# A recurrence in groups of two in place of four, half of its normalising on POOL, statistics of x carried in rows, and half of x loaded in the head

## The chip, the cores and the metric

The kernel runs on one core of a Trainium2 chip. The metric is the device time of one execution in microseconds, the median of several. Engines are named as in the profile: PE (TensorE, with PEld its weight loads), DVE (VectorE), ACT (ScalarE), POOL (GpSimd) and SP (SyncE, which here only issues transfers).

## The reference

x has 8 sequences of 512 tokens with 128 channels, 4096 tokens. All is float32. Three sublayers follow one another:

```
x = x + 0.5 * moe(layernorm(x))
x = x + ssm(layernorm(x))
x = x + 0.5 * moe(layernorm(x))

moe:  probs = softmax(tokens @ gate_w)            # 8 experts
      e = argmax(probs); pos = place of the token among those of expert e
      tokens with pos < 160 go through relu(t @ w1[e]) @ w2[e], times probs[e]; the others give 0
ssm:  h[t] = W h[t-1] + B u[t]     # W: a rotation, circulant, its eigenvalues of modulus 1 from a_params
      y[t] = C h[t] + D * u[t]
```

An expert's weights are 128 x 512 and 512 x 128. At most 8 x 160 = 1280 tokens are changed by a moe sublayer, ten tiles of 128 rows.

## The kernel before

**Head (to about 25 us).** SP issues loads in order: x turned (channels on partitions) for the gates, then small weights, w1, w2. PE computes the gate's logits, DVE picks each token's expert and numbers the tokens (`mark`, `number`, `encode`), and `index` (L734) turns that into `tok`, the ten tiles' token numbers. DVE also works out the rotation's angles (`eigenvalues`) and, later, tables of their multiples by doubling (`powers`, L561; a level is four small operations in a chain).

**Experts, `slots(n)`, n = 0 and 1.** POOL gathers ten tiles of rows into `xg` (L370), one indirect transfer after another, and later scatters ten tiles of `xnew` (L381). Each engine follows a list of steps written out by hand (L271 to L284), and takes them strictly in order:

- PE: `i` transposes a gathered tile, `l` multiplies it with the gate (n = 0), `u` is an expert's first product, `d` its second, `o` transposes a tile of outputs back, `t` and `s` are the last expert's second product straight into rows; `x` are matmuls that only keep PE's clock up.
- DVE: `i` takes a tile's statistics, `l` and `f` are the two halves of the softmax, `d` copies an expert's output to SBUF, `o` writes `xnew` = output x gate + `xg` (L794), `p` is a level of `powers`.
- ACT: `i` copies a transposed tile, `u` is the relu, `g` and `e` are the logarithm and exponentials of the softmax.

In n = 0 there is one softmax for all ten tiles; in n = 1 two groups of five. Row tiles of outputs go to PSUM banks 2 and 3 in turn (`row_bank`). Meanwhile SP copies x to a scratch tensor `x1_scratch` in DRAM, one sequence after each gather (L305); the scatter writes the changed rows over it; then SP loads all of it into `x1` (L309).

**Recurrence.** The state is kept in the basis where W turns pairs of numbers by an angle, so that a sequence's recurrence becomes a running sum between a turn back and a turn forth. Tokens are taken in groups of TB = 4 neighbours (token 4p + c lies in row p, tile c), so that the sum runs over 128 groups. Per sequence b:

- DVE: `stats` (four `bn_stats`, four aggregations), `shift`; ACT: `deviation`; ACT normalises four tiles into `u` (L520); for b = 0 and 1 ACT takes two tiles and DVE two (L897).
- PE: `turn_u` transposes `u` (L1149), ACT copies it to `uT` (two buffers, L502); `group_sums` (L1158) sums each group in the eigenbasis into bank 5.
- ACT copies the two half planes crosswise to `vq` (L494, L495); DVE multiplies bank 5 with cosines into `va` (L842), POOL `vq` with sines into `vb` (L402); DVE scans their sum into `z` (L850); DVE and POOL turn forth, `zs` (L853) and `zc` (L409), and DVE adds them into `state` (L862).
- PE: `within_pairs` and `within_rest` (L1169 to L1184) add what tokens of the same group give each other, seven tables of 136 columns for the lags 0 to 3 and some gate columns; `read_out` (L1192) adds what the carried state gives. 128 channels and 8 gate columns per token leave together.
- DVE: `add_back` and `gate_back` (L867 to L881) add x and give the logits for the second moe; SP stores rows and output.

PE works in software pipeline: group sums of sequence i, read-out of i - 1, first half of within i, transposes of i + 1, second half of within i. DVE routes the first half of the tokens for the second moe during sequences 4 to 6 (`mark`, `number`, `encode`), the rest at the end (`gate_first` and after); `place` (L1031) and `index` close the stage. The last sequence's gate columns are computed ahead (`gates_within`, L1211, `gates_carried`, L1217).

Of the kernel before, what the change touches and what calls it, by code (L numbers as in the profile page):

```python
# [5 lines left out]
def macaron_moe_ssm_kernel(nc, x_in, x_turned, a_params, b_w, c_w, c_w_turned, d_skip, gate_w, w1, w2,  # L6
# [12 lines left out]
    NB, SEQ, D = x_in.shape  # L19
    E, _, F = w1.shape  # L20
# [3 lines left out]
    NG = SEQ // TB  # L24
    PITCH = D + E
    NT = T // P
# [20 lines left out]
    with ctx:  # L47
# [48 lines left out]
        x1 = sb("x1", [P, NT, D])  # L96
# [46 lines left out]
        xnew = sb("xnew", [P, NS, D])  # L143

        om = sb("om", [P, 4])
        c1 = sb("c1", [P, TB + 1])
        s1 = sb("s1", [P, TB + 1])
# [3 lines left out]
        xj = sb("xj", [P, TB, D])  # L151
        xj_part = sb("xj_part", [P, TB, D])
        vt = sb("vt", [P, TB, P])
        gg = sb("gg", [P, 2, PITCH])
        gt_part = sb("gt_part", [P, TB, PITCH])
        gt = sb("gt", [P, TB, PITCH])
        eye_gate = sb("eye_gate", [P, PITCH])
        tab = sb("tab", [P, E + TB * PITCH])
        tab0 = sb("tab0", [P, PITCH + E])
        lgu = sb("lgu", [P, TB, E])  # L160
        sstat = sb("sstat", [P, 2, TB, 6])
        smv = sb("smv", [P, 2, TB, 2])
        sln = sb("sln", [P, 2, TB])
        ssd = sb("ssd", [P, 4, TB])
        srs = sb("srs", [P, 2, TB])
        snb = sb("snb", [P, 2, TB])
        u = sb("u", [P, 2, TB, D])
        uT = sb("uT", [P, 2, SEQ])
        tg = sb("tg", [P, TB, 2, TB * E])
        vq = sb("vq", [P, NG])  # L170
        va = sb("va", [P, NG])
# [3 lines left out]
        zs = sb("zs", [P, NG])  # L175
        state = sb("state", [P, 2, NG])

        x1_dram = nc.dram_tensor("x1_scratch", [T, D], F32, kind="Internal").ap()
# [15 lines left out]
        d_fill = sem("d_fill")  # L194
        d_gather = [sem(f"d_gather{j}") for j in range(NS)]
# [46 lines left out]
        def y_of(b):  # L242

            return y_pair(b)[:, :, E:E + 2 * PITCH].rearrange("p h (r c) -> p h r c", c=PITCH)
# [7 lines left out]
        def row_bank(i):  # L252

            return 1 if i == NS - 1 else 2 + i % 2
# [10 lines left out]
        GROUPS = [[(0, NS)], [(0, NS // 2), (NS // 2, NS)]]  # L265

        def group(n, i):
# [3 lines left out]
        pe_steps = [steps("i0 x1 i1 x2 u0 i2 l0 l1 d0 i3 u1 i4 l2 u2 i5 l3 d1 i6 l4 l5 u3 i7 i8 l6 "  # L271
                         "l7 i9 l8 l9 d2 u4 o0 o1 d3 u5 o2 o3 d4 o4 u6 o5 d5 u7 o6 d6 t8 o7 s8 o8 t9"),
                    steps("i0 x1 i1 x2 u0 i2 u1 i3 d0 i4 u2 i5 d1 o0 i6 u3 o1 i7 d2 "
                         "u4 o2 d3 i8 i9 u5 o3 o4 d4 u6 o5 d5 u7 o6 d6 t8 o7 s8 o8 t9")]

        dve_steps = [steps("i0 i1 i2 i3 i4 d0 i5 i6 i7 i8 d1 i9 l0 f0 d2 "
# [55 lines left out]
        def _(pool):  # L332
# [82 lines left out]
            for i in range(NB):  # L415
                turn_other_half(i)
                turn_cosine(i)
# [887 lines left out]
```

## Time and profile before

| | us |
|---|---|
| median of 3 runs (150.52 to 151.72) | 150.57 |
| the profiled execution | 152.99 |
| its span | 151.1 |

| engine | busy us | share of the span | instructions |
|---|---|---|---|
| PE | 131.5 | 87% | 753 |
| PEld | 99.0 | 66% | 753 |
| DVE | 87.4 | 58% | 378 |
| ACT | 56.7 | 38% | 157 |
| POOL | 56.1 | 37% | 96 |

The span is the time from the first to the last instruction of the profiled execution; its mean granted PE clock was 0.959 of full. Busy shares are averages over stages of different kinds. A busy PE includes matmuls that only keep its clock up (61 of them, 19.0 us). In a timeline a group's duration counts to the end of its last instruction; where matmuls overlap, the start of the next group tells better how long PE was taken.

### The profile page before, as it was taken

How to read it: one execution, taken by the hardware profiler on the slowest of the kernel's cores; microseconds unless marked ns; L12 is line 12 of the kernel's file. 1: busy time of each engine (PE TensorE's matmuls, PEld its weight loads, DVE VectorE, ACT ScalarE, POOL GpSimd, SP SyncE). 2: the span in 40 equal slices, each digit the busy share in tenths (PEclk: the TensorE clock that was granted, in tenths of full speed). 3: DMA queues.
4: the chain of work that ended last, by engine and by line, in shares of the span. 5: the costliest groups of instructions: out<-in, count | busy, mean ns of one | idle time of the engine just before them, and what ended most of it. 6: DMA issues, size and time to landing. Idle time of an engine off the chain costs nothing.

```text
span 151.1 us, 2503 instructions
## 1 busy us (share of the span) xinstructions
PE 131.5 (87%) x753; PEld 99.0 (66%) x753; DVE 87.4 (58%) x378; ACT 56.7 (38%) x157; POOL 56.1 (37%) x96
## 2 busy tenths in 40 slices
PE   5898989699589998788999999999999979999920
PEld 2315324298589987236877887788888349999810
DVE  1197778984354631165697669899894033855310
ACT  2522435135243323035576756673030035554200
POOL 3490003777002777401122112211200577575570
PEclk9999999999968999999999999999996599999997
DMA  3999994268700111394004413443116222211110
GB/s 83 298 368 389 347 290 121 56 181 248 226 22 0 56 56 52 78 314 181 7 0 143 133 41 117 143 136 104 49 41 201 68 55 55 55 40 36 35 52 17
DMA packets 15740, 18.49 MB, mean 122 GB/s; under 512 B 1904, under 2 KB 10608, under 8 KB 15600
## 3 DMA queue, kind: packets, MB, share of 16 engines
q1 hardware_dynamic: 13936, 15.34, 32.1%
q0 software_dynamic: 1280, 2.66, 6.4%
q10 hardware_dynamic: 512, 0.34, 0.8%
q8 instruction: 6, 0.10, 0.3%
q14 instruction: 6, 0.05, 0.1%
HBM read 12.70 MB, written 7.73 MB: 135 GB/s over the span
## 4 chain that ended last, share of the span: by engine, by line
PE 50%; DMA 13%; issue 9%; ACT 9%; POOL 7%; SPq 4%; DVE 4%; POOLq 1%
PE pair L1062 9%; PE pair L1075 9%; ACT u L520 7%; PE pair L1158 5%; DMA w1s<-w 5%; POOL xg L370 5%; PE pair L1149 3%; DMA xg<-x,tok 3%; PE pair L1180 3%; SPq L292 2%; PE pair L1182 2%; PE pair L1031 2%; PE pair L943 2%; PE pair L1087 2%; DMA x<-x_scratch 2%
## 5 line engine op out<-in xcount | busy, mean ns | idle before, releaser
L943 PE MATMUL pair<-warm_in,ones_bf 128*128 128x512 bf16 x61 | 19.0, 460 | 3.3 <-DMA x<-x_scratch 1.7
L1062 PE MATMUL pair<-xcT,w1s 128*128 128x160 f32 x128 | 21.3, 312 | 0.6 <-ACT xcT L452 0.6
L1062 PEld LDWEIGHTS pair<-xcT,w1s 128*128 128x128 f32 x128 | 19.0, 199 | 1.7 <-ACT xcT L452 1.7
L460 ACT ACTIVATE hT<-pair 128x320 f32<-128x320 f32 x32 | 13.8, 435 | 15.3 <-PE pair L1062 13.9
L1075 PE MATMUL pair<-hT,w2s 128*128 128x160 f32 x112 | 18.6, 312 | 0.2 <-ACT hT L460 0.2
L1075 PEld LDWEIGHTS pair<-hT,w2s 128*128 128x128 f32 x112 | 16.3, 197 | 0.2 <-issue 0.2
L370 POOL DMA_INDIRECT xg<-x,tok x10 | 10.2, 1020 | 16.7 <-issue 16.7
L370 POOL DMA_INDIRECT xg<-x_scratch,tok x10 | 10.1, 1010 | 13.4 <-DVE tok L743 10.7
L381 POOL DMA_INDIRECT x_scratch<-xnew,tok x10 | 9.9, 986 | 13.0 <-DVE xnew L794 10.8
L943 PEld LDWEIGHTS pair<-warm_in,ones_bf 128*128 128x128 bf16 x61 | 6.8, 117 | 11.6 <-issue 4.2
L402 POOL TENSOR_TENSOR vb<-vq,st 128x128 f32<-128x128 f32 x8 | 3.8, 475 | 26.7 <-ACT vq L495 26.7
L452 ACT COPY xcT<-pair 128x128 f32<-128x128 f32 x20 | 5.2, 264 | 20.4 <-PE pair L1046 20.4
L750 DVE BATCH_NORM_STATS2 gstat<-xg 128x6 f32<-128x128 f32 x20 | 5.7, 287 | 12.2 <-DMA xg<-x_scratch,tok 6.8
L381 POOL DMA_INDIRECT out<-xnew,tok x10 | 9.9, 989 | 6.6 <-DVE xnew L794 4.6
L520 ACT ACTIVATE u<-x,snb,srs 128x128 f32<-128x128 f32 x28 | 11.6, 482 | 0.4 <-DVE snb L833 0.2
L794 DVE SCALAR_TENSOR_TENSOR xnew<-pair,gscale,xg 128x128 f32<-128x128 f32 x20 | 6.6, 345 | 7.7 <-PE pair L1099 6.6
L1046 PE MATMUL pair<-ce,xg 128*128 128x128 f32 x20 | 5.8, 299 | 3.8 <-DMA xg<-x,tok 3.2
L1158 PE MATMUL pair<-uT,vt 128*128 128x128 f32 x64 | 8.5, 276 | 0.7 <-ACT uT L502 0.7
L817 DVE BATCH_NORM_STATS2 sstat<-x 128x6 f32<-128x128 f32 x32 | 6.9, 279 | 3.8 <-DMA x<-x_scratch 3.8
L1192 PE MATMUL pair<-gt,state 128*128 128x272 f32 x32 | 8.7, 393 | 0.0
L1158 PEld LDWEIGHTS pair<-uT,vt 128*128 128x128 f32 x64 | 7.8, 191 | 0.9 <-ACT uT L502 0.9
L409 POOL TENSOR_TENSOR zc<-z,ct 128x128 f32<-128x128 f32 x8 | 4.5, 561 | 9.8 <-DVE z L850 9.8
(190 smaller groups left out, 244.1 us busy)
## 6 DMA issues: line engine op xcount, KB each, us to landing
x_scratch<-x SPq DMA_DIRECT2D x8, 272.0 KB, 2.1
xt<-x_turned SPq DMA_DIRECT2D x8, 256.0 KB, 6.0
w1s<-w SPq DMA_DIRECT2D x2, 1024.0 KB, 8.6
w2s<-w SPq DMA_DIRECT2D x8, 256.0 KB, 6.7
x_scratch<-x SPq DMA_DIRECT2D x8, 256.0 KB
x<-x_scratch SPq DMA_DIRECT2D x8, 256.0 KB, 4.6
out<-x SPq DMA_DIRECT2D x8, 256.0 KB, 2.6
ce<-const_early ACTq DMA_DIRECT2D x1, 330.0 KB, 4.6
```

The lines of the kernel that those rows point to most:

```text
L370: pool.indirect_dma_start((xg[:, j, 0:D], xg[:, j, :])[n], None, (x_rows, x2_dram)[n], bass.IndirectOffsetOnAxis(ap=tok[:, j:j + 1], axis= ...
L381: pool.indirect_dma_start((x1_dram, out_rows)[n], bass.IndirectOffsetOnAxis(ap=tok[:, j:j + 1], axis=0), xnew[:, j, :], None, bounds_check ...
L460: nc.scalar.activation(hT[:, e % 2, half * HC:(half + 1) * HC, :], bank[4 + half][:, 0:HC * CAP] .rearrange("p (c s) -> p c s", c=HC), ACT ...
L520: ins = nc.scalar.activation(u[:, b % 2, c, :], x1[:, b * TB + c, :], ACT.Identity, bias=snb[:, b % 2, c:c + 1], scale=srs[:, b % 2, c:c + 1])
L794: V.scalar_tensor_tensor(xnew[:, i, :], bank[row_bank(i)][:, 0:P], gscale[:, i:i + 1], xg[:, i, 0:D], ALU.mult, ALU.add).then_inc(row_sb, 1)
L817: ins = V.bn_stats(sstat[:, b % 2, c, :], x1[:, b * TB + c, :])
L943: M(bank[to][:, :], ones_bf[:, :], warm_in[:, :], start=True, stop=True)
L1046: nc.tensor.transpose(bank[i % 2][:, 0:P], xg[:, i, 0:D], ident)\
L1062: ins = M(bank[4 + half][:, c * CAP:(c + 1) * CAP], w1s[:, i, ch * P:(ch + 1) * P], xcT[:, i * CAP:(i + 1) * CAP], start=True, stop=True)
L1075: ins = M(bank[6 + i % 2][:, 0:CAP], w2s[:, i, c, :], hT[:, i % 2, c, :], start=(c == 0), stop=(c == FC - 1))
L1158: ins = M(bank[5][:, 0:NG], vt[:, TB - 1 - c, :], uT[:, b % 2, c * P:(c + 1) * P], start=(c == 0), stop=(c == TB - 1))
L1192: ins = M(y[:, h, E:E + 2 * PITCH], state[:, b % 2, :], gt[:, 2 * h:2 * h + 2, :].rearrange("p r c -> p (r c)"), start=False, stop=True, s ...
```

## The change

- Groups have TR = 2 tokens, 256 groups per sequence. Lags and tables shrink (`tab` has two blocks of 144 columns, `tab0` goes), the state and all that is scanned get 256 columns. Group sums are two matmuls of 256 columns that read `uT` with a stride, in place of four of 128.
- `va` is written back into its PSUM bank. A copy of the sines (`st_near`) and `zs` lie in PSUM bank 7. The next group sums wait for `z`, as do `gates_within`.
- `within(b, h)` and `read_out(b, h)` go by halves and come one sequence later, on both sides of `turn_u`; `uT` has three buffers.
- From sequence 2 on ACT normalises two tiles and POOL the other two (`normalise_other`, after `zc`).
- `x1` and `xnew` get rows of 134 columns: 128 of data and 6 of `bn_stats`. In the first experts SP loads x into SBUF, DVE takes its statistics there (steps `x`), SP stores the longer rows to the scratch tensor; after each `o` DVE takes the statistics of `xnew`, and the scatter waits for those. After the reload only the aggregation is left; deviations are taken in four groups of tiles.
- SP's order: four of eight w2 loads, four of eight x loads, then with waits on gathers 3 and 4 the other x loads with stores of the first four, then the other stores behind gathers 5 to 8, then the other w2 loads.
- The first softmax has two groups of five tiles. All levels of `powers` for the tables move behind the last rows (`p0` to `p7`). Rows 0 to 4 of n = 0 all use bank 3.
- The ends of both lists are reordered; there are fewer warming matmuls ahead of the recurrence.

```diff
+    TR = 2
+    NG = SEQ // TR
+    XP = D + 6
...
+        st_near, zs = bank[7][:, 0:NG], bank[7][:, NG:2 * NG]
...
-                         "l7 i9 l8 l9 d2 u4 o0 o1 d3 u5 o2 o3 d4 o4 u6 o5 d5 u7 o6 d6 t8 o7 s8 o8 t9"),
+        pe_steps = [steps("i0 x1 i1 x2 u0 i2 l0 l1 d0 i3 u1 i4 l2 l3 u2 l4 i5 d1 o0 i6 l5 u3 o1 i7 "
+                         "l6 d2 i8 l7 u4 o2 i9 l8 d3 l9 o3 u5 o4 d4 u6 o5 d5 d6 o6 u7 o7 t8 s8 o8 t9"),
                     steps("i0 x1 i1 x2 u0 i2 u1 i3 d0 i4 u2 i5 d1 o0 i6 u3 o1 i7 d2 "
-                         "u4 o2 d3 i8 i9 u5 o3 o4 d4 u6 o5 d5 u7 o6 d6 t8 o7 s8 o8 t9")]
-        dve_steps = [steps("i0 i1 i2 i3 i4 d0 i5 i6 i7 i8 d1 i9 l0 f0 d2 "
-                         "o0 o1 d3 p5 o2 o3 d4 p6 o4 o5 d5 o6 d6 o7 o8 o9"),
+                         "u4 o2 d3 i8 i9 u5 o3 o4 d4 u6 o5 d5 d6 o6 u7 o7 t8 s8 o8 t9")]
+        dve_steps = [steps("x0 x1 i0 x2 i1 x3 i2 i3 i4 d0 l0 i5 f0 x4 x5 d1 x6 i6 x7 o0 i7 o1 d2 i8 "
+                         "o2 i9 d3 l1 o3 f1 o4 p0 p1 d4 p2 o5 p3 d5 d6 o6 p4 o7 o8 o9 p5 p6 p7"),
...
+            for e in range(E // 2):
+                load_w2(e)
+            for b in range(NB // 2):
+                load_x(b)
+            for b in range(NB // 2, NB):
+                sp.wait_ge(d_gather[3 + (b - NB // 2) // 2], 16)
+                load_x(b)
+                store_x(b - NB // 2)
+            for b in range(NB // 2, NB):
                 sp.wait_ge(d_gather[b + 1], 16)
-                sp.dma_start(tiles(x1_dram, b), tiles(x_rows, b)).then_inc(d_fill, 16)
+                store_x(b)
+            for e in range(E // 2, E):
+                load_w2(e)
...
+            def normalise_other(b):
+                pool.wait_ge(snb_r, rated_with(b) + 1)
+                pool.wait_ge(uT_ps, b - 1)
+                for c in range(TB // 2, TB):
+                    t = b * TB + c
+                    ins = nc.gpsimd.tensor_scalar(u[:, b % 2, c, :], x1[:, t, 0:D], srs[:, t:t + 1], snb[:, t:t + 1],
+                                                  ALU.mult, ALU.add)
+                ins.then_inc(u_pool, 1)
...
                 turn_other_half(i)
                 turn_cosine(i)
+                if i + 2 < NB:
+                    normalise_other(i + 2)
...
+                def rate_rows(b):
+                    dve.wait_ge(d_x1[b], 16)
+                    for t in range(b * TB, (b + 1) * TB):
+                        ins = V.bn_stats(x1[:, t, D:XP], x1[:, t, 0:D])
+                    ins.then_inc(x_rated, 1)
...
+                        if n == 0:
+                            dve.wait_ge(row_sb, i + 1)
+                            V.bn_stats(xnew[:, i, D:XP], xnew[:, i, 0:D]).then_inc(row_rated, 1)
...
-            powers(ct, st, 0, 5)
...
-                V.tensor_tensor(va[:, :], bank[5][:, 0:NG], ct[:, 0:NG], ALU.mult).then_inc(va_r, 1)
+                V.tensor_tensor(bank[5][:, 0:NG], bank[5][:, 0:NG], ct[:, 0:NG], ALU.mult).then_inc(va_r, 1)
...
+                        if n == 0 and 1 <= i <= NS // 2:
+                            pe.wait_ge(row_sb, i)
...
-            keep_warm(16, 7)
-            pe.wait_ge(d_x1[0], 16)
-            keep_warm(14, 7)
+            keep_warm(16, 6)
+            pe.wait_ge(d_x1[0], 32)
+            keep_warm(9, 6)
...
+            for i in range(NB):
                 group_sums(i)
                 if i >= 1:
-                    read_out(i - 1)
-                within_pairs(i)
-                turn_u(i + 1)
+                    within(i - 1, 0)
+                    read_out(i - 1, 0)
+                if i < LAST:
+                    turn_u(i + 1)
+                if i >= 1:
+                    within(i - 1, 1)
+                    read_out(i - 1, 1)
                 if i == NB // 2 + 2:
                     rank(1, 0)
-                within_rest(i)
...
             gates_within(LAST)
+            within(LAST, 0)
             gates_carried(LAST)
-            within_rest(LAST)
-            read_out(LAST)
+            within(LAST, 1)
+            for h in range(2):
+                read_out(LAST, h)
```

## Rows read from the trace of the kernel before

**Rows 1.** The chain of waits in order of time: start us, us, what.
```profile
42.90 2.06 PE pair L1075 x8
...
59.84 2.24 DMA x_scratch<-xnew,tok
...
62.16 2.74 DMA x<-x_scratch
...
64.95 3.20 PE pair L943 x14
...
104.36 0.89 PE pair L1158 x8
...
107.34 0.84 PE pair L1211 x8
...
116.38 0.17 DVE unfilled L736
```

**Rows 2.** Stretches: length, busy of PE PEld DVE ACT POOL, PE clock, DMA share, GB/s.
```profile
40.00:42.00 2.00, 0.45 (x5) 0.36 (x4) 0.48 (x3) 0.22 (x1) 0.00 (x0) 1.00 0.78 266
43.00:46.00 3.00, 3.00 (x13) 3.00 (x13) 1.67 (x7) 0.82 (x3) 0.00 (x0) 0.51 0.00 0
```

**Rows 3.** PE in order of time, third expert and one period.
```profile
34.50 1.33 PE L1062 MATMUL pair<-xcT,w1s 128*128 128x160 f32 x8
...
78.89 1.05 PE L1158 MATMUL pair<-uT,vt 128*128 128x128 f32 x8
79.79 1.08 PE L1192 MATMUL pair<-gt,state 128*128 128x272 f32 x4
80.70 0.64 PE L1169 MATMUL pair<-tab,uT 128*128 128x280 f32 x2
...
82.25 0.66 PE L1149 MATMUL pair<-ce,u 128*128 128x128 f32 x4 [0.20 <-ACT u L520]
82.74 0.62 PE L1180 MATMUL pair<-tab,uT 128*128 128x272 f32 x2
...
83.92 1.05 PE L1158 MATMUL pair<-uT,vt 128*128 128x128 f32 x8
```

**Rows 4.** Stretches of DVE: softmax; a doubling; state to gates; choosing; numbering.
```profile
42.98:44.82 1.84, 1.34 (x6) 0.52 0.00 0
48.43:49.29 0.86, 0.80 (x5) 1.00 0.00 0
78.22:79.48 1.26, 1.23 (x5) 1.00 0.00 0
99.59:100.94 1.35, 1.25 (x7) 1.00 0.37 137
103.80:105.92 2.12, 1.92 (x10) 1.00 0.56 187
```

**Rows 5.** DVE by form: busy us, mean ns of one, idle before.
```profile
L817 DVE BATCH_NORM_STATS2 sstat<-x 128x6 f32<-128x128 f32 x32 | 6.9, 279 | 3.8 <-DMA x<-x_scratch 3.8
L794 DVE SCALAR_TENSOR_TENSOR xnew<-pair,gscale,xg 128x128 f32<-128x128 f32 x20 | 6.6, 345 | 7.7 <-PE pair L1099 6.6 <-PE pair L1087 1.1
L853 DVE TENSOR_TENSOR zs<-z,st 64x128 f32<-64x128 f32 x16 | 5.9, 369 | 0.4
L670 DVE TENSOR_TENSOR_SCAN counted<-restart,chosen 128x256 bf16<-128x256 bf16 x1 | 0.7, 691 | 0.0
L686 DVE TENSOR_TENSOR own_count<-pair,chosen 128x256 f32<-128x256 f32 x1 | 0.4, 426 | 0.6 <-PE pair L1006 0.6
```

**Rows 6.** POOL by form, same columns.
```profile
L409 POOL TENSOR_TENSOR zc<-z,ct 128x128 f32<-128x128 f32 x8 | 4.5, 561 | 9.8 <-DVE z L850 9.8
L402 POOL TENSOR_TENSOR vb<-vq,st 128x128 f32<-128x128 f32 x8 | 3.8, 475 | 26.7 <-ACT vq L495 26.7
L358 POOL COPY eye_gate<-ce 128x128 f32<-128x128 f32 x1 | 0.3, 285 | 0.0
```

**Rows 7.** ACT by form, same columns.
```profile
L486 ACT COPY tab<-pair 128x272 f32<-128x272 f32 x1 | 0.4, 391 | 0.0
```

**Rows 8.** POOL in order of time, the end.
```profile
145.29 0.98 POOL L381 DMA_INDIRECT out<-xnew,tok  x1 [0.30 <-issue]
```

More of the change, by code:

```diff
@@ L528, in _ @@
             turned_part(0)
-            normalise(1)
+            normalise(1, 0, TB // 2)
+            deviation(2)
             for i in range(NB):
@@ L861, in turn_forth @@
                     dve.wait_ge(y_ps, b - 1)
-                V.tensor_tensor(state[:, b % 2, :], zc[:, :], zs[:, :], ALU.add).then_inc(state_r, 1)
+                V.tensor_tensor(state_out(b), by_group(zc), by_group(zs), ALU.add).then_inc(state_r, 1)
             def add_back(b):
@@ L1133, in _ @@
             pe.wait_ge(gg_sb, 1)
-            for k in range(TB):
+            for k in range(TR):
                 ins = nc.tensor.transpose(bank[5][:, k * P:(k + 1) * P], xj[:, k, :], ident)
             ins.then_inc(vt_ps, 1)
-            for k in range(TB):
-                at_ = k % 2 * PITCH
-                ins = M(bank[4 + 2 * (k // 2)][:, at_:at_ + PITCH], xj[:, k, :], gg[:, 0, :], start=True, stop=True)
+            for k in range(TR):
+                ins = M(bank[4][:, k * PITCH:(k + 1) * PITCH], xj[:, k, :], gg[:, 0, :], start=True, stop=True)
             ins.then_inc(k_ps, 1)
@@ L1155, in group_sums, with within @@
                 if b >= 1:
-                    pe.wait_ge(va_r, b)
-                for c in range(TB):
-                    ins = M(bank[5][:, 0:NG], vt[:, TB - 1 - c, :],
-                            uT[:, b % 2, c * P:(c + 1) * P], start=(c == 0), stop=(c == TB - 1))
+                    pe.wait_ge(z_r, b)
+                by_residue = uT[:, b % 3, :].rearrange("d (h r p) -> d r p h", h=2, r=TR)
+                for r in range(TR):
+                    ins = M(bank[5][:, 0:NG].rearrange("s (p h) -> s p h", h=2), vt[:, TR - 1 - r, :],
+                            by_residue[:, r, :, :], start=(r == 0), stop=(r == TR - 1))
                 ins.then_inc(v_ps, 1)
-            def within_pairs(b):
-                if b >= 2:
+            def within(b, h):
+                if b >= 2 and h == 0:
                     pe.wait_ge(x2_r, b - 1)
@@ L1187, in read_out @@
-            def read_out(b):
-                pe.wait_ge(state_r, b + 1)
-                y = y_pair(b)
-                for h in range(2):
-                    ins = M(y[:, h, E:E + 2 * PITCH], state[:, b % 2, :],
-                            gt[:, 2 * h:2 * h + 2, :].rearrange("p r c -> p (r c)"), start=False, stop=True,
-                            skip_group_check=True)
-                ins.then_inc(y_ps, 1)
+                M(y[:, h, 0:TR * BLOCK], uT[:, b % 3, 2 * h * P:(2 * h + 1) * P], tab[:, :, :].rearrange("p r c -> p (r c)"),
+                  start=True, stop=False, skip_group_check=True)
```

300 lines of the change are left out of this document (152 added, 148 removed).

## Prediction

> **What bounds the kernel now.** I read the chain that ended last first, then the granted clock by stretch, then each engine's order in time, then the duration of each form of instruction. The chain shows five stages. Up to about 25 us is the head; the change shortens a few VectorE operations there that end before what they feed, so it counts as nothing. From 25 to 59.84 the first experts run, and the stage's last scatter starts at 59.84; 2.24 us later it has landed, and 2.74 us after that the first rows are back at 64.9 [rows 1]. From there the recurrence runs until the token index begins at 116.38, and the second experts take the rest.
>
> The recurrence repeats every 5.03 us (78.89 to 83.92), and TensorE leaves only some 0.35 us of it free [rows 3]. The free piece is a wait for ScalarE's `u`. So the period is nearly TensorE's own work, and only less work there shortens it much.
>
> In the first experts TensorE was busy 0.45 us of the two before 42, waiting for gathered rows, and then found its clock halved: 0.51 of full from 43 to 46, and the eight matmuls that start at 42.90 took 2.06 us [rows 1, 2].
>
> **Recurrence, the period.** Seven tables of columns per batch become four: 2 x (288 + 144) = 864 columns in place of 1392. Today's last three, 696 columns, take 1.18 us (82.74 to 83.92), 1.70 ns each, so 864 take 1.47. The group sums stream 512 columns before and after, 0.90; read-out 0.91 and the transposes 0.49 stay. TensorE's period becomes 3.77 us [rows 3]. The others must fit under it:
> - ScalarE: one copy of 512 columns, two of the four `u`, two `vq` of 256 columns, at most 0.39 each by the 272-column copy [rows 7]: no more than 2.5 us in all, by the pieces that it had.
> - VectorE, from one `z` to the next: two `zs`, then state, add and gates, then `va`, then the scan. The 256-column row with an operand in PSUM is 0.43, the 256-column scan 0.69 [rows 5]; state, add and gates took 1.26 for 128 states [rows 4], 0.13 more for 256. With `zs` at 0.43 each and 0.04 for each of four hand-overs: 0.86 + 1.39 + 0.43 + 0.69 + 0.16 = 3.5 us.
> - POOL: `vb` and `zc`, 0.475 and 0.561 at 128 columns [rows 6]. Taking the 0.285 copy's two ends, I put the wider ones at 0.77 and 0.8 to 0.95. Its two normalises per batch have no row: below, the one-input copy, 0.285; above, the two-input 0.561. I take 0.4, as they have one tensor input. With the scan between: 0.9 + 0.8 + 0.77 + 0.75 + 0.2 = 3.4 us.
>
> `zs` is the term with two answers. Its 64 x 128 form takes 0.369 [rows 5], longer than a full-height operation with one operand in PSUM would, and it runs beside POOL's `zc`. The change puts its table and its result into PSUM. If that does not help, twice 0.369 is 0.74 for each. I take 0.43, the nearest row in width and placement. By the Trainium skill, GPSIMD Engine Reference, section Specifications, POOL and VectorE share SBUF interfaces and collide when VectorE reads two SBUF inputs; by that rule `zs` and `zc` both get cheaper. If the rule were not what costs here, the VectorE loop would be 4.15 us and the sum some 2.5 us worse. The trace agrees only so far that `zc`, beside `zs`, is slower than `vb`.
>
> **Recurrence, start.** Four `bn_stats` (0.22 each back to back) leave the front, and the warm matmuls after the first arrival go from 14 in 3.20 us to 9, 2.06 [rows 1]: the first transposes start 2.25 us after the arrival in place of 3.3, a gain of 1.05.
>
> **Recurrence, walk.** Times after the first arrival: group sums of batches 0, 1, 2 start at 3.6, 7.6, 12.0 (the first two gaps are set by ScalarE's `vq`, the scan, and the extra statistics on VectorE), then every 3.77 until batch 6 at 27.1. From batch 4 on VectorE also routes the first half of the tokens. Choosing takes 1.35 and numbering with encoding 2.12 [rows 4], and no `bn_stats` any longer drops out to make room. So `z` of batch 5 is there at 27.0, of batch 6 at 27.0 + 3.5 + 1.35 = 31.85, of batch 7 at 31.85 + 3.5 + 2.12 = 37.5. Because `va` now stays in its bank, the gates of the last batch wait for the last of these; TensorE is through at 35.1 and stands still 2.3 us. From the gates to the index took 9.04 (107.34 to 116.38) [rows 1]; two within halves, 1.47, take the place of 1.18, one more small matmul pair is some 0.25, and the last hot parts come 0.3 late: 9.9. Index at 47.4; before, 116.38 - 64.9 = 51.5. The loop from first to last group sums gives 6.5, the tail takes 3.5 back, and with the start the stage gains **4.1**.
>
> **First experts.** Here VectorE gets work: 32 statistics of x (about 0.9 for a batch of four, 0.279 each alone), one after each of ten output rows, and five doublings of the turn tables, 0.86 each for the shape shown [rows 4, 5]. Before, the doublings stood under the wait for the first gathers. Two batches of x stand there now, and two more fit between the next arrivals. The other four do not. The third expert's first matmuls start at 34.5 [rows 3], two small logit products later now, so the first softmax may begin at 36.0. In VectorE's order follow: softmax with its exponential, 1.84 at ten tiles [rows 4]; four batches of x, 3.6; a copy, 0.35; a gathered tile's statistics, 0.4, or later in that wait; the first row, 0.345 [rows 5]. That is 42.5. The rows of the first half share one bank, so the second row's transpose waits for the first row, and TensorE, in order, has nothing past 39.5. It stands still for 3.0 us where it had waited for gathers, so the half clock of 43 to 46 [rows 2] stays, and the matmuls that started at 42.90 start at 43.0, with some 0.85 us of tile transposes and logits still to come.
>
> After that: second softmax done at 51.5 (its exponential stands behind the relu of expert 5), a row, two doublings and the fourth copy until 54.1, for which row 5's transpose and all behind it wait from 52.3; then two more products, three doublings, three rows, the last expert and the ends follow, the last product at 60.3, its row and statistics 60.95. The last three rows come faster than POOL can scatter them, 1.28 us each by the 0.98 and 0.30 of the row at 145.29 [rows 8], so the last scatter starts at 62.6: a loss of **2.7**. Bounds: 0.8 if the clock is not halved, 5 if the late loads of x come 2 us after VectorE wants them.
>
> SP's queue: half of the w2 loads, half of the x loads before any wait; then the other x loads and stores behind gathers 3 and 4, stores behind 5 to 8 and the statistics of the batch, and the other half of w2 last, issued near 43. Its first user is expert 4's second product near 50, so 7 us cover it. If the stores hung, w2, the first scatter (it needs all stores) and the reload would hang with them. Rows of 134 in place of 128 columns cost the reload 5% of 2.74, **0.1** [rows 1].
>
> **Second experts.** The only edit is that the end's order puts row 7 ahead of the last expert's partial product. At 145.29 the scatter of row 8 waited for nothing but POOL itself [rows 8]: row 7 0.6 us earlier moves the last three. Gain **0.6**.
>
> **Sum**: -4.1 + 2.7 + 0.1 - 0.6 = -1.9 us against the profiled execution's 152.99 (span 151.1 and 1.9 around it). That execution lies 2.4 above the median, 150.57; the difference carries over: **148.7 us**.
>
> **Rivals.**
> 1. The clock falls in the recurrence as well. TensorE idles 3.1 of 4.7 us at the start (2.9 to 7.6 after arrival) and 2.3 in one piece before the last gates; 0.45 busy of 2 came before the fall seen [rows 2]. One fall costs about 1.9 (the 2.06 against 1.09 of an undisturbed block, twice). Against: at the start today the idle pieces cost no clock. One fall gives 150.6, two give 152.5, less where VectorE is late anyway. Chance 0.27, mostly one.
> 2. POOL becomes the bound: slower. The two normalises sit between `zc` and the next `vb`; from 0.55 us each POOL's loop passes 3.77, and at 0.9 each it is 4.4, at 1.2 it is 5.0, and the six later periods lose 4 to 7 us: 152.5 to 156. It decides from 0.75 each (loop 4.1, the whole gain gone). For it: no such instruction is in the trace. Against: copies of this size take 0.285 [rows 6]. Chance 0.12.
> 3. No half clock in the first experts, or the wait there shorter, since the stall is now one block behind dense work: -1.9 to -3: 145.5 to 147. Chance 0.18.
> 4. The statistics do not fit as walked, late x loads or w2: 151 to 153. Chance 0.13.
>
> **Numbers.** The forecast, 147 to 150, has 0.30. One per cent, 1.5 us, is about what can be told from no change. Faster by over that (under 149.1): two thirds of the forecast and rival 3, with a share of a half-fall, 0.42. Slower (over 152.1): rival 2, half of 4, double falls, 0.24. Between: 0.34. The range 144.8 to 153 takes in rival 3 with a cheaper VectorE and rival 4, and leaves the worse half of rival 2 out.
>
> **What would show it.** Period of group sums near 3.8 from batch 2, then 4.6 or more for the last; TensorE idle 2 us before the last gates; `zs` near 0.43, POOL's normalise near 0.4; TensorE idle around 39.5 to 42.5 with `xnew` as releaser; the last first-stage scatter near 62.6; first transposes 2.25 after the arrival. Wrong would be: a first-row wait under 1 us, gathers or x loads as its releaser, a POOL pair over 1.5 us, or a clock at half in the recurrence.

## The result, and the profile after

The changed kernel takes 156.11 us (median of 4 runs, 155.43 to 157.15), the kernel before beside it 151.14 (150.52 to 153.04): ratio 1.030, 95% interval 1.023 to 1.037. It is slower; 148.7 was forecast, in a range up to 153.0. Ratios here are between runs within 1.5% of a kernel's fastest; since the kernel before ran from 149.33 to 156.01 with its mean granted clock between 0.978 and 0.902, medians of all runs are given beside them.

The profiled execution took 157.15, its span 155.3. From the chain of waits after (start us, us, what):

```profile
64.58 2.33 DMA x_scratch<-xnew,tok
66.97 2.76 DMA x<-x_scratch
69.78 3.64 PE pair L999 x9
...
121.09 0.17 DVE unfilled L786
```

Against [rows 1] the last scatter of the first experts is 4.74 later (64.58 for 59.84), where 2.7 was expected. From the arrival (69.73) to the index is 51.36 for 51.5, where 47.4 was expected. The last part, from the index to the end of the span, went from 34.7 to 34.2, as forecast. The nine matmuls that should take 2.06 took 3.64. The granted clock by stretch tells why (PE's busy us, PE clock, DMA share, GB/s):

```profile
42.00:49.00 7.00, 5.72 (x23) 0.51 0.88 275
...
69.50:73.00 3.50, 3.22 (x8) 0.51 1.00 347
79.50:83.50 4.00, 4.00 (x14) 0.57 0.00 0
110.00:112.00 2.00, 0.85 (x8) 1.00 0.12 36
```

At three places it is near one half, the 1.2 of its two levels (1.2 and 2.4 GHz). In [rows 2] there is one of them, half as long. (All kernels here but e3 have one more fall around the index, from 114.5 in the kernel before and 120.5 after; with it, the time from the index to the end is 34.2 to 34.7 us in every one, so it is left out of the account.) What TensorE did before each fall, and one period of the recurrence, stand in its order of time (last column: idle before, and releaser):

```profile
43.28 0.45 PE L1159 MATMUL pair<-ce,eoT 128*128 128x128 f32 x1 [3.17 <-DVE xnew L852]
...
44.02 2.48 PE L1133 MATMUL pair<-hT,w2s 128*128 128x160 f32 x8
...
69.78 3.64 PE L999 MATMUL pair<-warm_in,ones_bf 128*128 128x512 bf16 x9 [2.50 <-DMA x<-x_scratch]
73.26 0.60 PE L1210 MATMUL pair<-ce,u 128*128 128x128 f32 x4
...
77.62 0.66 PE L1210 MATMUL pair<-ce,u 128*128 128x128 f32 x4 [1.74 <-ACT u L570]
78.95 1.60 PE L1220 MATMUL pair<-uT,vt 128*128 128x256 f32 x4 [0.68 <-ACT uT L554]
...
84.55 1.25 PE L1220 MATMUL pair<-uT,vt 128*128 128x256 f32 x4
85.63 0.65 PE L1230 MATMUL pair<-tab,uT 128*128 128x288 f32 x2
...
88.45 1.25 PE L1220 MATMUL pair<-uT,vt 128*128 128x256 f32 x4
...
111.15 1.05 PE L1260 MATMUL pair<-tg,uT 128*128 128x32 f32 x8 [1.97 <-DVE z L904]
```

An idle piece of 3.17, one of 2.50, and pieces of 0.67, 1.74 and 0.68 around the first two group sums stand ahead of the falls; the 1.97 before the last gates has none behind it. The kernel before has shorter pieces around its first group sums, because `within` of the first sequence stood between those sums and the next transposes:

```profile
69.52 1.16 PE L1158 MATMUL pair<-uT,vt 128*128 128x128 f32 x8 [0.68 <-ACT uT L502]
...
72.20 0.66 PE L1149 MATMUL pair<-ce,u 128*128 128x128 f32 x4 [0.35 <-ACT u L520]
```

The period is 3.90 (84.55 to 88.45) in place of 5.03 [rows 3]; 3.77 was forecast. The group sums hold TensorE 1.08 (84.55 to 85.63), not 0.90. The terms that had no row before are now there (mean ns of one, by form on VectorE, then on POOL):

```profile
L907 DVE TENSOR_TENSOR pair<-z,pair 64x256 f32<-64x256 f32 x16 | 6.9, 430 | 0.4
L916 DVE TENSOR_TENSOR state<-zc,pair 128x256 f32<-128x256 f32 x8 | 4.9, 609 | 0.2
```

```profile
L443 POOL TENSOR_TENSOR vb<-vq,st 128x256 f32<-128x256 f32 x8 | 5.9, 733 | 16.3 <-ACT vq L547 16.3
L450 POOL TENSOR_TENSOR zc<-z,ct 128x256 f32<-128x256 f32 x8 | 5.8, 724 | 10.4 <-DVE z L904 10.4
L458 POOL TENSOR_SCALAR u<-x,srs,snb 128x128 f32<-128x128 f32 x12 | 5.3, 447 | 0.3 <-DVE snb L887 0.3
```

`zs` is 0.43 and POOL's normalise 0.447, about as taken (0.43 and 0.4); `vb` and `zc` are under the 0.77 and 0.9 taken; `state` is over. It takes 0.609, where 0.42 was allowed: its 0.292 at half the width, from the trace of before, and 0.13.

### The profile page after: what moved, and what is told of

Same layout as the page of the kernel before. It is cut to its first block, busy times and chain, and to the rows that moved or that the text cites. A ratio compares the mean times of both kernels' runs of the same rounds, so it can differ in the third digit from the quotient of the medians.

```text
span 155.3 us, 2344 instructions
## 1 busy us (share of the span) xinstructions
PE 125.9 (81%) x677; PEld 92.4 (59%) x680; DVE 94.3 (61%) x375; ACT 51.4 (33%) x135; POOL 63.8 (41%) x104
## 4 chain that ended last, share of the span: by engine, by line
PE 36%; DMA 16%; issue 16%; DVE 11%; POOL 10%; SPq 6%; ACT 2%; POOLq 1%; DVEq 0%
PE pair L1120 9%; PE pair L1133 9%; DMA w1s<-w 5%; DMA x<-x 4%; POOL u L458 3%; POOL vb L443 3%; PE pair L999 3%; PE pair L1145 3%; PE pair L1087 2%; SPq L314 2%; PE pair L1159 2%; DMA x<-x_scratch 2%; POOL zc L450 2%; DMA xg<-x_scratch,tok 2%; DMA xg<-x,tok 2%
## 5 line engine op out<-in xcount | busy, mean ns | idle before, releaser
L999 PE MATMUL pair<-warm_in,ones_bf 128*128 128x512 bf16 x53 | 17.3, 475 | 4.5 <-DMA x<-x_scratch 2.5
L409 POOL DMA_INDIRECT xg<-x_scratch,tok x10 | 10.1, 1009 | 13.8 <-DVE tok L793 11.1
L443 POOL TENSOR_TENSOR vb<-vq,st 128x256 f32<-128x256 f32 x8 | 5.9, 733 | 16.3 <-ACT vq L547 16.3
L1220 PE MATMUL pair<-uT,vt 128*128 128x256 f32 x32 | 10.6, 454 | 2.3 <-ACT uT L554 1.4
L1230 PE MATMUL pair<-tab,uT 128*128 128x288 f32 x32 | 11.1, 429 | 0.0
L1240 PE MATMUL pair<-gt,state 128*128 128x272 f32 x32 | 10.3, 409 | 0.0
L450 POOL TENSOR_TENSOR zc<-z,ct 128x256 f32<-128x256 f32 x8 | 5.8, 724 | 10.4 <-DVE z L904 10.4
L1159 PE MATMUL pair<-ce,eoT 128*128 128x128 f32 (+1 forms) x18 | 5.2, 296 | 5.0 <-DVE xnew L852 3.2
L1220 PEld LDWEIGHTS pair<-uT,vt 128*128 128x128 f32 x32 | 5.7, 189 | 4.9 <-ACT uT L554 1.8
```

Of the source, the lines that this page charges most:

```text
L409: pool.indirect_dma_start((xg[:, j, 0:D], xg[:, j, :])[n], None, (x_rows, x2_dram)[n], bass.IndirectOffsetOnAxis(ap=tok[:, j:j + 1], axis= ...
L443: nc.gpsimd.tensor_tensor(vb[:, :], vq[:, :], st[:, 0:NG], ALU.mult).then_inc(vb_r, 1)
L450: nc.gpsimd.tensor_tensor(zc[:, :], z[:, 0:NG], ct[:, 0:NG], ALU.mult).then_inc(zc_r, 1)
L999: M(bank[to][:, :], ones_bf[:, :], warm_in[:, :], start=True, stop=True)
L1159: nc.tensor.transpose(bank[row_bank(n, i)][0:s1 - i * P, 0:P], eoT[:, i * P:s1], ident)\
L1220: ins = M(bank[5][:, 0:NG].rearrange("s (p h) -> s p h", h=2), vt[:, TR - 1 - r, :], by_residue[:, r, :, :], start=(r == 0), stop=(r == TR ...
```

## The experiments

All runs stand in this table; times within a run are us of its profiled execution. "Falls" are stretches at half clock from 30 us on, without the one around the index; "scatter" is the start of the first experts' last one, "arrival" the end of the first reload in the chain, "2 to 3" the time from the second to the third group sums.

| run | falls | scatter | arrival to transposes | 2 to 3 | arrival to index | span | median | ratio (95%) |
|---|---|---|---|---|---|---|---|---|
| before | 43-46.5 | 59.84 | 3.32 | 5.01 | 51.5 | 151.1 | 151.14 | |
| after | 42-49, 69.5-73, 79.5-83.5 | 64.58 | 3.53 | 5.60 | 51.4 | 155.3 | 156.11 | 1.030 (1.023-1.037) |
| e1_warm_reload | 43-47, 74-81 | 62.71 | 2.45 | 5.92 | 51.1 | 153.2 | 155.55 | 1.021 (1.006-1.037) |
| e2_warm_rows | 72.5-79.5 | 61.20 | 2.41 | 5.92 | 51.1 | 151.7 | 154.80 | 1.024 (1.013-1.036) |
| e3_head_before | 68.5-79, 113-120 | 58.02 | 3.31 | 6.40 | 61.8 | 160.6 | 162.12 | |
| e4_stats_late | 66.5-70.5, 77-80.5 | 62.02 | 3.52 | 5.59 | 51.3 | 152.8 | 155.64 | 1.024 (1.006-1.042) |
| e7_warm_all | none | 61.53 | 2.42 | 4.00 | 48.7 | 149.6 | 152.77 | 1.016 (0.997-1.036) |
| e8_warm_tail | none | 60.37 | 2.40 | 4.00 | 48.2 | 147.9 | 149.87 | 0.999 (0.994-1.003) |
| e9_warm_act | 105.5-113 | 61.12 | 2.41 | 4.61 | 52.5 | 152.9 | 154.25 | 1.026 (1.008-1.045) |
| e10_before_warm | none | 58.20 | 3.32 | 5.02 | 51.5 | 149.5 | 151.29 | 1.010 (1.003-1.018) |
| e11_plain_order | 106-110 | 61.39 | 2.41 | 3.83 | 49.2 | 149.8 | 152.04 | 1.002 (0.994-1.011) |
| e12_one_stat | 41.5-48.5, 109.5-113.5 | 63.67 | 2.42 | 4.00 | 50.1 | 153.4 | 154.87 | 1.029 (1.022-1.037) |
| e13_one_stat_late | 43.5-47.5, 105-112.5 | 61.05 | 2.80 | 4.00 | 52.2 | 152.6 | 152.71 | 1.015 (1.007-1.023) |
| e14_loads_first | 42.5-46, 107-111 | 62.21 | 2.42 | 3.99 | 50.1 | 151.7 | 154.65 | |
| e15_loads_one_stat | 105-108.5 | 59.30 | 2.41 | 4.00 | 50.1 | 148.8 | 150.37 | |
| e16_one_late | none | 61.02 | 2.41 | 3.99 | 48.2 | 148.4 | 151.09 | |

Medians of the kernel before beside them: 152.37 (e1 to e4), 152.41 (e7 to e10), 152.17 (e11 to e13), 154.07 (e14 to e16).

**Is it the clock?** Theory: each fall costs 1.5 to 2 us, and the three of them are what is missing. Rival: the work itself is longer, and the slow matmuls hide in waits.

```diff
-            keep_warm(16, 6)
+            keep_warm(27, 6)          # e1: the reload
```


> 27 warming matmuls instead of 16 ahead of the reload, so that TensorE does not idle the 2.5 us before the first rows of x are back; nothing else changes. Clock theory (the idle piece lets the granted clock fall, and the recurrence starts at half rate): the nine warm matmuls after the arrival take 2.1 us in place of 3.64, the first transposes start 2.3 us after the arrival in place of 3.7, and the total falls by 1.4, or by up to 2.7 if the second fall, near 80 us, goes too: 153.4 to 154.7 against 156.1. Rival (the start waits for u, and a slow clock hides behind that): within 0.5 us of the changed kernel.

```diff
-  ... o0 i6 l5 u3 o1 i7
+  ... o0 i6 l5 u3 w24 o1 i7           # e2: 24 warming matmuls of 256 columns
```


> 24 half-width warming matmuls (256 columns, into an unused part of a bank) where TensorE stands 3.2 us before the second output row of the first experts. Clock theory: row one comes as late as before, at 43.3, but the two products behind it take 1.1 us each in place of 2.3, the second softmax is done some 2.3 us earlier, and the last scatter starts at 62.3 in place of 64.6: total 153.7 to 154.3. Rival (VectorE's chain of statistics, doublings and rows sets the end of the stage whatever the clock): less than 0.7 us gained.

Each filled the gap that it was meant for: transposes 2.45 after the arrival in e1, and no fall in the first experts in e2. But the clock then fell in the recurrence's start, for 7 us in both, and 2 to 3 became longer, 5.92; neither median came down to its forecast (155.55 for 153.4 to 154.7, 154.80 for 153.7 to 154.3). Two things vary that the edits did not touch. In e1 the fall of the first experts lasted 4 us in place of 7, and their scatter came 1.87 earlier. In e2 the idle piece of the reload was still there, and the clock stayed at full behind it:

```profile
66.48 2.12 PE L999 MATMUL pair<-warm_in,ones_bf 128*128 128x512 bf16 x9 [2.57 <-DMA x<-x_scratch]
```

So which piece costs a fall, and for how long, the piece alone does not settle. A third filling was added (`keep_warm` of 2 after the first transposes, 7 after the first group sums, 2 before the second):

> All three stretches in which the clock fell are filled with matmuls that compute nothing: 24 half-width ones ahead of the second row's transpose, 27 full-width ones in the reload in place of 16, and 2, 7 and 2 in the gaps around the first two group sums. Theory (the missing 4 us are the granted clock): no fall between 42 and 112 us; last first-stage scatter 61.2, first transposes 68.8, second to third group sums 4.4 to 4.7 us in place of 5.6, index near 116.2, span near 150.3, ratio to the kernel before 1.00 to 1.01. Rival (the change's own work is too long and the falls hide in waits anyway): the third group sums wait for VectorE's scan where they waited for a slow TensorE, 5.5 us or more between them, index stays at 117.5, ratio 1.02 or more.

The clock over the same stretches and the whole start (columns as above), e7:

```profile
42.00:49.00 7.00, 6.53 (x52) 1.00 0.95 296
66.00:70.00 4.00, 3.65 (x18) 1.00 0.90 268
70.00:84.00 14.00, 13.23 (x62) 1.00 0.29 103
```

and its first transposes and third group sums (TensorE in order of time):

```profile
69.07 0.63 PE L1213 MATMUL pair<-ce,u 128*128 128x128 f32 x4 [0.26 <-ACT u L570]
...
78.79 1.24 PE L1223 MATMUL pair<-uT,vt 128*128 128x256 f32 x4
```

No fall is left but the one around the index, and the span is shorter by 5.7. From the two profiles: the last scatter comes 3.05 earlier (61.53 for 64.58), the transposes after the arrival 1.11 (2.42 for 3.53), the third group sums after the transposes 1.57 (9.72 for 11.29); from there to the index both take 36.5 (36.53 and 36.54). That is 5.73 of 5.7, all of it at the three falls. For this pair of profiles the theory holds. The runs of this kernel spread from 151.25 to 155.07 with a mean clock of 0.977 to 0.952, so the filling does not keep the clock in every one; its interval takes in no change.

The same was done to the kernel before, 13 matmuls in its wait for the last gathered tile:

> The kernel before with 13 half-width matmuls that compute nothing, in TensorE's wait for the last gathered tile at 40.3 to 41.8. Theory (each fall costs what its slow matmuls cost): the fall of 43 to 46.5 goes, the last first-stage scatter comes 1 to 2 us earlier than 59.84, span 149.2 to 150, ratio 0.987 to 0.995. Rival: VectorE's rows set that stage's end, and the fall costs nothing: ratio 1.00 and the scatter at 59.8.

Its fall went too, and the last scatter came 1.64 earlier. The same product, TensorE in order of time, before and in e10:

```profile
42.75 2.20 PE L1075 MATMUL pair<-hT,w2s 128*128 128x160 f32 x8
```

```profile
42.77 1.33 PE L1078 MATMUL pair<-hT,w2s 128*128 128x160 f32 x8
```

Its median, 151.29, lies below 152.41, but the ratio is 1.010 (1.003 to 1.018), where 0.987 to 0.995 was expected, so the times do not show that the filling pays. With full clock the two kernels compare as follows, e7 less e10: first experts +3.33, recurrence -2.9 (48.7 for 51.5), index to end -0.5 (34.3 for 34.7), span +0.1. Without its falls the change is worth nothing by these spans, and by the two medians e7 is 1.5 longer (152.77 for 151.29); -1.9 was forecast.

**What holds the first row?** TensorE's 3.17 us wait is for VectorE's first row, which stands behind the statistics of x. VectorE in order of time, after:

```profile
40.31 0.87 DVE L806 BATCH_NORM_STATS2 x<-x 128x6 f32<-128x128 f32 x4 [0.43 <-DMA x<-x]
...
42.01 0.87 DVE L806 BATCH_NORM_STATS2 x<-x 128x6 f32<-128x128 f32 x4 [0.41 <-DMA x<-x]
42.80 0.34 DVE L852 SCALAR_TENSOR_TENSOR xnew<-pair,gscale,xg 128x128 f32<-128x128 f32 x1
```

First the last four batches' statistics were moved behind two rows (`x4 x5` behind `o1`, `x6` behind `i8`, `x7` behind `i9`, the second half of w2 ahead of the late stores):

> The last four batches' statistics of x move behind the first two output rows, into gaps that VectorE had there (2.1 and 2.1 us), and the other half of w2 is loaded ahead of the late stores. Theory that VectorE's place for the statistics makes the stall: row one comes near 39.7 in place of 42.9, TensorE's wait falls from 3.2 to under 1 us, the clock does not fall there, the last scatter starts at 61.6 (POOL's ten scatters behind the last store become the bound): total 152.5 to 153.5. Rival (the stall is the late arrival of x, or the clock falls all the same): the last scatter within 1 us of 64.6.

The wait went, and with it the fall, but the last scatter started at 62.02, 3.6 after the last row (58.39): POOL's ten scatters, 1.29 each without a gap from 50.37, wait for all eight stores, and the last of these was issued only at 46.4. TensorE's idle piece in the reload grew to 4.39, the clock fell there, and the median is 155.64, not 152.5 to 153.5. Then twelve of the sixteen late statistics were left out, with and without the first doublings moved behind the fourth copy:

```diff
-   for t in range(b * TB, (b + 1) * TB):
+   for t in range(b * TB, (b + 1) * TB if b < NB // 2 else b * TB + 1):   # e12
-   f1 o4 p0 p1 d4 p2 o5 p3 d5 d6 o6 p4 o7
+   f1 o4 d4 p0 o5 p1 d5 d6 o6 p2 o7 o8 o9 p3 p4                           # e13 as well
```


> The reload and the start of the recurrence filled, the wait of the second row not; of the last four batches of x only one tile of four has its statistics taken in the first experts (the other twelve hold a constant, so later values are not the reference's). Theory (VectorE's statistics of x make the wait that lets the clock fall there): 12 x 0.22 = 2.6 us less on VectorE, the wait ahead of the second row's transpose 3.2 goes to under 1, no fall at 42, last scatter near 59.5 in place of 64.6 (61.5 with the wait filled). Rival (the late loads of x and the first softmax make it): the wait stays over 2 and the clock falls, last scatter 63 or later.

> The same as the one with one tile's statistics of four, and the first doublings of the turn tables behind the fourth copy of an expert's output. If statistics and doublings on VectorE are all that the first experts lost: the waits of 3.2 and 1.5 both gone, last scatter 58.2 to 58.7, where the kernel before without its fall has 58.2; span near 146.5. Rival (the order of the ends, the ten statistics of rows or POOL's scatters cost as well): 59.5 or later.

The theory fell: TensorE's wait for the first row stayed at 2.95 in both. In e12:

```profile
42.05 0.45 PE L1160 MATMUL pair<-ce,eoT 128*128 128x128 f32 x1 [2.95 <-DVE xnew L852]
```

VectorE had less to do and waited longer for x instead:

```profile
39.56 0.29 DVE L806 BATCH_NORM_STATS2 x<-x 128x6 f32<-128x128 f32 x1 [1.02 <-DMA x<-x]
...
41.36 0.29 DVE L806 BATCH_NORM_STATS2 x<-x 128x6 f32<-128x128 f32 x1 [1.10 <-DMA x<-x]
41.57 0.33 DVE L852 SCALAR_TENSOR_TENSOR xnew<-pair,gscale,xg 128x128 f32<-128x128 f32 x1
```

Each late load of x is paired in SP's queue with a store, while the gathers run. So the loads were put one behind the other, with all statistics (e14) and with one of four (e15):

```diff
             for b in range(NB // 2, NB):
                 sp.wait_ge(d_gather[3 + (b - NB // 2) // 2], 16)
                 load_x(b)
-                store_x(b - NB // 2)
+            for b in range(NB // 2):
+                store_x(b)
```


> The reload and the start of the recurrence filled; in SP's queue the last four loads of x go out one behind the other, each no longer paired with a store of the first four, and all statistics stay. If the transfers alone hold the first row: VectorE's waits for x (0.43 and 0.41) go, TensorE's wait ahead of the second row's transpose falls to about 2.3, last scatter 63. If VectorE's work would hold it as long by itself: the wait stays 2.8 to 3.2 and the clock falls at 42 again, last scatter 63.5 to 64.6. Neither expects under 1.

> The loads ahead of the stores and, of the last four batches of x, one tile's statistics of four (a constant in the rest, so later values are not the reference's). If it takes both, transfers and VectorE's statistics, to hold the first row, either being enough: TensorE's wait ahead of the second row's transpose goes from 2.95 to under 1.2, no fall at 42, last scatter 59.5 to 60.5. If something third holds it (the first softmax, ScalarE's exponential): the wait stays over 2 and the clock falls, last scatter 63 or more.

VectorE's statistics and first row, then TensorE's wait for that row, in e14:

```profile
39.52 0.86 DVE L807 BATCH_NORM_STATS2 x<-x 128x6 f32<-128x128 f32 x4
...
40.71 0.84 DVE L807 BATCH_NORM_STATS2 x<-x 128x6 f32<-128x128 f32 x4
41.46 0.34 DVE L853 SCALAR_TENSOR_TENSOR xnew<-pair,gscale,xg 128x128 f32<-128x128 f32 x1
```

```profile
41.95 0.30 PE L1160 MATMUL pair<-ce,eoT 128*128 128x128 f32 x1 [3.17 <-DVE xnew L853]
```

and in e15:

```profile
39.47 0.34 DVE L853 SCALAR_TENSOR_TENSOR xnew<-pair,gscale,xg 128x128 f32<-128x128 f32 x1
```

```profile
39.95 0.30 PE L1161 MATMUL pair<-ce,eoT 128*128 128x128 f32 x1 [0.38 <-DVE xnew L853]
...
48.84 1.35 PE L1135 MATMUL pair<-hT,w2s 128*128 128x160 f32 x8 [1.65 <-DMA w2s<-w]
```

Four kernels settle it: TensorE's wait is 3.17 as changed, 2.95 with less VectorE work, 3.17 with quicker loads (VectorE then has no wait for x in it), 0.38 with both. The row itself moves a little with either: counted from the softmax's last operation on VectorE it starts 4.27 to 5.17 later in the seven runs that leave this part of VectorE's and SP's order as changed, 4.27 and 4.14 with less VectorE work, 3.93 with quicker loads, 1.76 with both. So either holds the row nearly as long by itself; only both together free it, and only then the fall goes and the scatter comes at 59.30. What is late next shows as well: w2, 1.65.

**The period.** Group sums now read neighbours of two halves in turn, 1024 bytes apart, and `state` is written so, 512 bytes apart. In e11 both are in plain order (groups are then scanned in another order, so values differ from the reference's), on top of e7:

```diff
-   by_residue = uT[...].rearrange("d (h r p) -> d r p h", h=2, r=TR)
+   by_residue = uT[...].rearrange("d (h r p) -> d r h p", h=2, r=TR)
-   state[:, b % 2, :].rearrange("s (h p) -> s p h", h=2)
+   state[:, b % 2, :].rearrange("s (h p) -> s h p", h=2)     # bank 5, zc and zs likewise
```


> All gaps filled as before, and the groups of a batch in plain order: the group sums read their 256 columns in runs of 128 and not 512 bytes apart between neighbours of two halves, and the state is read and written in the same order. The groups are then scanned in another order than the reference's, so the values are not its. If the interleaved order is what made the group sums 1.08 us in place of 0.90 and the state operation 0.61 in place of 0.43: period 3.72 in place of 3.90, seven of them 1.3 us, index 1.3 to 1.8 us earlier after the arrival (46.9 to 47.4 in place of 48.7), span 148. Rival (the width of 256 columns, or the operands' places, make both): 3.90 and 0.61 stay, span 149.6.

TensorE in order of time, e11:

```profile
85.51 1.03 PE L1223 MATMUL pair<-uT,vt 128*128 128x256 f32 x4
86.38 0.65 PE L1233 MATMUL pair<-tab,uT 128*128 128x288 f32 x2
...
89.19 1.03 PE L1223 MATMUL pair<-uT,vt 128*128 128x256 f32 x4
```

and VectorE by form:

```profile
L916 DVE TENSOR_TENSOR state<-zc,pair 128x256 f32<-128x256 f32 x8 | 3.4, 420 | 0.2
```

The group sums hold TensorE 0.87 in place of 1.08, the period is 3.68, `state` 0.420 in place of 0.606. By the seventh group sums, 26.96 after the arrival, 1.2 is gained on e7 (28.15), where the forecast had 27.1. The last two sums wait for `z` longer (0.95 for 0.63), so 0.9 is left at the gates; behind them the clock fell in this run, so its index is no measure. By the Trainium skill, SBUF - State Buffer, section Door 1, SBUF works in lines of 16 bytes, and accesses that go to another line each time pay for it. The trace agrees that the interleaved order is what costs, 0.19 per `state` and 0.21 per group sums; the line's size no run here shows.

**POOL's half.** In e9 ScalarE normalises all four tiles (on top of e7):

```diff
-                if i + 2 < NB:
-                    normalise_other(i + 2)
...
-                    normalise(i + 2, 0, TB // 2)
+                    normalise(i + 2, 0, TB)
```


> The same filled gaps, with ScalarE normalising all four tiles of a batch from the third on, and POOL none. Theory (TensorE sets the period, POOL's half is hidden and so is ScalarE's): period 3.90 as before, ScalarE at 4 x 0.39 + 0.39 + 2 x 0.37 = 2.7 us per batch, span within 0.4 of the kernel with filled gaps. Rival (ScalarE's two more tiles stand ahead of the copies that the scan waits for): period 4.3 or more, PE idle for z, +2.5 us.

```profile
78.89 1.32 PE L1219 MATMUL pair<-uT,vt 128*128 128x256 f32 x4 [0.44 <-DVE z L902]
```

Between the two: the third group sums wait 0.44 for `z`, from the fifth on the period is 3.90 again, and the last gates come 39.48 after the arrival in place of 38.73. POOL's half gains 0.75 us; the rest of e9's loss is a fall of 7.5 us behind the gates. `state` takes 0.606 there too, so it is not POOL's normalising that lengthens it.

**Carried statistics.** e3 joins the first experts of before to the changed recurrence, with the statistics taken on VectorE in each period:

> The first experts as in the kernel before (one softmax, copy of x from DRAM to DRAM, statistics of x taken on VectorE after the reload, doublings in their old place), the recurrence as in the changed kernel (groups of two, POOL normalising half). If the recurrence by itself pays and the loss lies in the first experts, the total is about 147: the last first scatter back at 59.8, a period of 3.9. My expectation: VectorE's loop gets its statistics back, 3.5 + 1.25 + 0.15 = 4.9 us, so the period is 4.9 and hardly better than 5.03, the tail stays 3.5 us longer than before, and the total is 152 to 154: the two halves of the change need each other.

It took 162.12 (158.42 to 166.84), not 152 to 154, with falls at 68.5 to 79 and 113 to 120. The rows of its loop between them (TensorE) show a chain that I had not walked, statistics between `va` and the scan:

```profile
90.03 1.32 PE L1191 MATMUL pair<-uT,vt 128*128 128x256 f32 x4 [1.22 <-DVE z L882]
95.57 1.32 PE L1191 MATMUL pair<-uT,vt 128*128 128x256 f32 x4 [1.22 <-DVE z L882]
```

A period of 5.54, longer than the 5.03 of before: groups of two need the statistics elsewhere.

**A better order.** e8 adds to e7 the doublings of e13 and the numbering behind the last state; e16 also has e14's loads, 14 warming matmuls for 24, `x7` behind `o1` and its store behind w2:

```diff
-                if i == NB // 2 + 2:
+                if i == LAST:
                     number(1, 0)
```


> The same filled gaps, and two moves in VectorE's order: the first five doublings of the turn tables behind the fourth copy of an expert's output instead of between row 4 and that copy, and numbering the first half of the tokens behind the last state instead of behind the one before it. If VectorE's order causes the two waits: TensorE's idle time of 0.9 to 1.5 before row 5 and of 1.97 before the last gates both fall under 0.5; last first-stage scatter 60.4 in place of 61.2, and the index comes 1.5 to 1.9 earlier after the arrival: span 147.8, ratio 0.98 to 0.99. Rival: the numbering only moves, its rank comes late for the hot parts and the index is no earlier, and POOL's scatters take up what the doublings give: span as with filled gaps alone, within 0.5.

> The correct kernel with everything learnt: the three stretches filled (14 half-width matmuls ahead of the second row in place of 24), the first doublings behind the fourth copy, the numbering behind the last state, the loads ahead of the stores, the last batch's statistics behind the second row and its store behind the second half of w2. If the first row is free by then: the wait ahead of its successor is filled whole by the 14, last scatter 59.4 in place of 60.4, index 112.7, span 147.0, ratio to the kernel before 0.985 to 0.995. Rival (POOL's ten scatters at 1.29 each start a microsecond later with the last store and take it back): last scatter 60.4 or later, span 147.9 or more.

e8 has 149.87 (12 runs, 148.99 to 150.46), against 152.41 for before (17 runs), 152.77 for e7 and 151.29 for e10 on the same chip: the shortest median, though the ratio to before is 0.999 where 0.98 to 0.99 was expected. The doublings gave 1.16. The numbering gave only 0.45 of the 1.5 expected: the 1.97 before the gates went, and TensorE waits later.

```profile
108.58 0.23 PE L1055 MATMUL pair<-counted,ones_bf 128*128 128x128 bf16 x1 [1.41 <-DVE counted L720]
```

From the last scan on VectorE has no wait in its rows until 111.9; it is the bound there, and TensorE's idle time was only where that showed. In e16 the first row is done by 41.0, but the rival held: POOL starts its scatters, 1.3 apart up to 61.02, once the last store has landed (the first of them, POOL in order of time).

```profile
49.31 1.03 POOL L426 DMA_INDIRECT x_scratch<-xnew,tok  x1 [11.49 <-DMA x_scratch<-x]
```

Its 151.09 stands against 154.07 for before on that chip; whether it beats e8 these runs, on different chips, do not tell.

## Why the prediction was wrong

By its own steps. The span rose by 4.2 where the sum said -1.9: 6.1 missed, 2.0 in the first experts, 4.0 in the recurrence, 0.1 in the last part.

- **The clock in the recurrence** is the step that failed. "At the start today the idle pieces cost no clock" was taken as grounds to leave rival 1 at 0.27 and out of the sum. But today's pieces at that place are 0.68 and 0.35; by moving `within` of the first sequence away, the change makes them 0.67, 1.74 and 0.68, as the prediction's own 3.1 of 4.7 us idle says. And the reload's idle piece, not among the places feared, grew from 1.73 to 2.50. Two falls, 1.11 and 1.57 (after against e7): 2.7 of the 4.0. The place that I feared as well, 2 us before the last gates, cost nothing in the profiled run, and that was luck: its idle time was there (1.97), and the same piece brought a fall in seven other runs.
- **The half clock in the first experts** "stays": it did, but for 7 us in place of 3.5. The loss of 2.7, with 0.8 if the clock is not halved, put that half clock at 1.9 and the last scatter without it at 60.6. The runs show 3.05 (after against e7) and 61.53; that gives the 2.0, 1.15 from the clock and 0.9 from the work. The 3.05 belongs to this one profile: with the same order in e1 the fall was 4 us long and cost 1.18 against e7.
- **The first row** was forecast for 42.5 and came at 42.80, TensorE's wait 3.0 and is 3.17, row 5's 1.8 and is 1.49. That is in part luck: I walked VectorE alone, and without its waits for x the row starts at 41.46 (e14); the loads of x, put into rival 4, hold it nearly as long (e12, e15).
- **The period**, 3.77 forecast: 3.90, from the group sums' interleaved read, taken as 0.90 "before and after". Without falls e7 still has 1.3 of the 4.0; plain order gives back 1.2 of it by the seventh sums and 0.9 by the gates (e11). `state` was mis-sized by 0.18 as well, off the path until the last two batches.
- **Right**: `zs` (0.430 for twice the columns that took 0.369 [rows 5]), now that its table and result lie in PSUM. By the Trainium skill, GPSIMD Engine Reference, section Specifications, POOL and VectorE collide when VectorE reads two SBUF inputs; the trace agrees so far that `zc`, beside `zs`, was 0.086 longer than `vb` before [rows 6] and no longer is (0.724 and 0.733). No run here changes the place alone, so the placement as the cause is argued and not shown. Right too: POOL's normalise (rival 2 falls), the last group sums to the index (15.6 for 15.5), reload (+0.1), second experts (-0.5 for -0.6).

Left open: how often, and why, the clock falls in the kernel before. Its one trace, of 152.99, shows the fall behind an idle piece of 1.55; e3, whose first experts are those of before, kept the full clock behind the same piece, and its last scatter came at 58.02, about where e10 has it (58.20). TensorE in order of time, e3:

```profile
41.65 0.33 PE L1077 MATMUL pair<-ce,xg 128*128 128x128 f32 x1 [1.64 <-DMA xg<-x,tok]
```

The spread of the kernel before, 149.33 to 156.01, goes with its mean clock only in part: 149.33 was taken at 0.977, but 151.95 at 0.976 and 154.07 at 0.973. What else lengthens those runs no trace here shows.

## What to carry to other kernels

A change that takes TensorE's work away, or moves it, without shortening what TensorE waits for turns dense stretches into stretches with gaps; compare each new gap with the old one at that place, price a fall of the clock behind it by what slow blocks cost there, and fill the gap in the same change. When one engine's order holds a step, walk the transfers that feed it to the same instant too: taking away one of two nearly equal causes shows next to nothing. Idle time of one engine ahead of a late step is worth what the bound engine gains, not its own length (1.97 us gave 0.45).

## What the runs showed of the hardware

- The same idle piece may or may not cost the clock. After 1.97 us before the last gates it stayed at full in after, e1, e2, e4 and e7, and fell in e3, e9 and e11 to e15, all with that piece (1.96 to 2.08). After some 2.5 us in the reload it was at half in after (2.50) and at full in e2 (2.57) and e16 (2.62); after some 1.6 us at the last gathered tile it was at half in before (1.55) and at full in e3 (1.64).
- With the same instructions a fall lasted 7 us in after and 4 us in e1. With one gap filled the next fall came sooner and lasted longer: 6.1 to 13.1 us after the arrival in e1 and e2, 9.8 to 13.8 in after.
- Interleaved 4-byte accesses cost TensorE's moving operand 0.21 us per group sums of 512 columns (1.08 for 0.87), and a VectorE write of 256 columns 0.19 (0.606 for 0.420).
- Twenty-four matmuls of 256 bf16 columns filled 2.78 us and kept the clock at 1.00 through 42 to 49 (e7).
